# Feed-forward rows of later groups: scaling moved from VectorE to GpSimd, turning moved from TensorE to VectorE by way of DRAM

## The reference, cut to what matters

```python
x = x + xattn(layernorm(x), ctx); x = x + attn(layernorm(x))
z = layernorm(x)                       # (x - mean) / sqrt(var + 1e-5), per row of 512 channels
h = fix8(z @ w1 + b1)                  # 2048 rows, 512 -> 2048; fix8 rounds to multiples of 1/256
h = fix8(interp(h, 33 points of GELU on [-4, 4]))   # 0 below -4, h above 4
x = x + fix8(h @ w2 + b2)              # 2048 -> 512
```

## Time and profile before

| | |
|---|---|
| median of three runs | 1586.72 us |
| the profiled execution | 1586.93 us |
| its span (first to last instruction) | 1585.0 us |
| granted TensorE clock, mean | 0.999 |
| busy PE, DVE, ACT, POOL | 99%, 79%, 64%, 52% of the span |
| the feed-forward layer's rounds | from about 1216 us to the end |

### The profile page before, as it was taken

How to read it: one execution, slowest core, us unless ns; L and a number is a source line. 1 busy time by engine, 2 the same in 40 slices (tenths; PEclk the granted TensorE clock), 3 DMA queues, 4 the chain that set the end, 5 groups by cost and what they waited for, 6 DMA issues and landing times. The chain is left out here.

```text
span 1585.0 us, 30386 instructions
## 1 busy us (share of the span) xinstructions
PE 1569.8 (99%) x11114; PEld 1377.5 (87%) x11114; DVE 1245.0 (79%) x2409; ACT 1021.1 (64%) x2025; POOL 822.0 (52%) x784
## 2 busy tenths in 40 slices
PE   9999999999999999999999999999999999999998
PEld 7889899898999989999899888988988887888886
DVE  6558878887888878878788685767777889989887
ACT  3457777777777777777787442445446666666765
POOL 3318657376573856747456242333334555555554
PEclk9999999999999999999999999999999999999999
DMA  8984636456364654635433684432436601011010
GB/s 253 271 258 150 180 111 189 127 169 176 117 185 120 178 164 128 187 108 152 139 112 95 186 284 137 136 90 81 139 96 222 244 14 61 20 36 39 7 54 27
DMA packets 203412, 215.60 MB, mean 136 GB/s; under 512 B 83776, under 2 KB 149632, under 8 KB 203264
## 3 DMA queue, kind: packets, MB, share of 16 engines
q1 hardware_dynamic: 203264, 213.66, 43.8%
HBM read 154.88 MB, written 58.72 MB: 135 GB/s over the span
## 5 line engine op out<-in xcount | busy, mean ns | idle before, releaser
L79 PE MATMUL p_bank_score<-p_ctxt,p_qo 128*128 128x256 f32 x2304 | 304.6, 286 | 0.8 <-ACT p_probs L1112 0.4
L79 PEld LDWEIGHTS p_bank_score<-p_ctxt,p_qo 128*128 128x128 f32 x2304 | 288.1, 191 | 5.9 <-issue 2.2
L79 PE MATMUL p_bank_mix<-p_probt,p_ctx 128*128 128x512 f32 x1152 | 292.0, 397 | 0.5
L79 PEld LDWEIGHTS p_bank_mix<-p_probt,p_ctx 128*128 128x128 f32 x1152 | 207.4, 189 | 41.8 <-issue 3.8
L1316 DVE SCALAR_TENSOR_TENSOR p_qo<-p_bank_mix,p_odd,p_qo 128x512 fp32r<-128x512 f32 x192 | 143.8, 749 | 57.6 <-ACT p_qo L1126 50.1
L1126 ACT ACTIVATE p_qo<-p_bank_mix,p_odd 128x512 fp32r<-128x512 f32 x192 | 132.4, 690 | 68.2 <-PE p_bank_mix L79 67.6
L1112 ACT ACTIVATE p_probs<-p_bank_score,p_small 128x257 f32<-128x257 f32 x256 | 121.5, 475 | 58.6 <-DVE p_small L1297 54.1
L801 POOL TENSOR_SCALAR p_probs<-p_probs,p_small 128x256 f32<-128x256 f32 x256 | 122.2, 485 | 68.9 <-DVE p_small L1303 68.8
L795 POOL TENSOR_TENSOR p_ctx<-p_ctx_in,p_ctx 128x768 fp32r<-128x768 f32 x64 | 118.5, 1851 | 66.7 <-ACT p_ctx L1101 66.4
L790 POOL TENSOR_TENSOR p_ctx_in<-p_ctx_in,p_odd_in 128x768 f32<-128x768 f32 x64 | 118.2, 1847 | 40.2 <-DMA p_odd_in<-in_ctx_dram 40.2
L1297 DVE TENSOR_REDUCE p_small<-p_bank_score 128x1 f32<-128x257 f32 x256 | 105.4, 415 | 10.2 <-PE p_bank_score L79 7.6
(11 more groups left out here) (302 smaller groups left out, 3917.4 us busy)
## 6 DMA issues: line engine op xcount, KB each, us to landing
p_blocks_in<-in_ctx_dram SPq DMA_DIRECT2D x256, 96.0 KB, 2.4
p_ctx_in<-in_ctx_dram SPq DMA_DIRECT2D x64, 384.0 KB, 3.1
q<-p_ctx SPq DMA_DIRECT2D x64, 256.0 KB, 3.7
ffn<-p_w_raw SPq DMA_DIRECT2D x64, 256.0 KB, 2.9
p_odd_in<-in_ctx_dram SPq DMA_DIRECT2D x64, 192.0 KB, 3.6
p_x<-in_x_dram SPq DMA_DIRECT2D x32, 256.0 KB, 4.1
p_quad<-q SPq DMA_DIRECT2D x32, 256.0 KB, 3.6
p_probt<-q SPq DMA_DIRECT2D x32, 256.0 KB, 3.8
```

Of the source, the lines that this page charges most:

```text
L79: made = e.matmul(out, lhsT, rhs, start=n == 0, stop=n == last)
```

## The change

For the tiles of the later groups:

- TensorE's `turn` is gone from its list.
- GpSimd scales tile j at f = 6 + 2j (SCALED is now 6), at the head of its round, that is behind the second product of the round before. It reads the tile channel by channel of each 32-row block (every fourth element) and writes the result in order, into one of the two tiles `sums` that hold the feed-forward sums at a group's end.
- SyncE writes that tile to DRAM at f = 6 + 2j and reads it back as 4 DMAs in blocks into the place of the loaded rows.
- VectorE no longer scales; it turns the blocks with one instruction at f = 8 + 2j (TURNED is now 8), ahead of `snap`. The reading order of that instruction is contiguous (`ordered=True`); in self-attention it reads every fourth element.
- `high` and `low` follow at f = 8 + 2j.
- The statistics are finished in the same round as before (FINISHED = 5).

```diff
-    def turn_blocks(self, e, i):
+    def turn_blocks(self, e, i, ordered=False):
...
-        e.transpose(bank.rearrange("p (k a r) -> p a k r", k=C // P, r=QUAD),
-                    z.rearrange("p (a j k) -> p a k j", k=C // P, j=QUAD)).then_inc(self.turned, 1)
+        blocks = z.rearrange("p (a k j) -> p a k j" if ordered else "p (a j k) -> p a k j", k=C // P, j=QUAD)
+        e.transpose(bank.rearrange("p (k a r) -> p a k r", k=C // P, r=QUAD), blocks).then_inc(self.turned, 1)
...
-        LOADED, SCALED, TURNED = 4, 5, 7
+        LOADED, FINISHED, SCALED, TURNED = 4, 5, 6, 8
...
             def put_row(kind, i):
...
-                e.dma_start(z_dram[at, i], scaled.home(i)).then_inc(done, DMA)
+                rows = sums[i % 2][:] if kind == "n" and i >= after.early else scaled.home(i)
+                e.dma_start(z_dram[at, i], rows).then_inc(done, DMA)
...
                 if n + 7 < KF:
                     load_block(n + 7)
+                for i in tile_at(n, SCALED):
+                    put_row("n", i)
+                    load_blocks("n", i)
...
+            def scale_ordered(i):
+                x_is_in(e, "z", i)
+                if i == after.early:
+                    e.wait_ge(after.norm.steps, 14)
+                if i >= 2 * NRF:
+                    e.wait_ge(out_done, NRF * (i // NRF - 1))
+                if i >= after.early + 2:
+                    e.wait_ge(n_put, DMA * (i - 1))
+                made = x_of("z", i).rearrange("p (a j k) -> p a k j", k=KT, j=QUAD)
+                e.tensor_scalar(sums[i % 2][:].rearrange("p (a k j) -> p a k j", k=KT, j=QUAD), made,
+                                after.norm.minus[:, i:i + 1], after.norm.inv[:, i:i + 1], ALU.add,
+                                ALU.mult).then_inc(after.norm.chain, 1)
...
             for n in range(1, NF):
+                for i in tile_at(n, SCALED):
+                    scale_ordered(i)
                 rest_by_slope(n)
...
                     if k < NF - 2:
                         down(k)
-                for i in tile_at(n, TURNED):
-                    after.norm.turn(e, i)
...
-                for i in tile_at(n, SCALED):
-                    scaled_rows(i)
+                for i in tile_at(n, TURNED):
+                    e.wait_ge(n_blocks[i % 2], NB * DMA * (i // 2 + 1))
+                    after.norm.turn_blocks(e, i, ordered=True)
                 snap(n)
                 for i in tile_at(n, TURNED):
                     after.norm.low(e, i, zts_next[(g + 1) % 2], i % NRF * P)
```

More of the change, by code:

```diff
@@ L2125, in scalar @@
                 g = n // KF
-                if n == SCALED - 1:
+                if n == FINISHED - 1:
                     after.norm.root(e, 1)
@@ L2212, in low_h @@
                                            op1=ALU.subtract).then_inc(h_lo, 1)
-            def scaled_rows(i):
-                x_is_in(e, "z", i)
-                after.norm.scale(e, i, x_of("z", i))
             def down_sum(i):
@@ L2330, in vector @@
                     after.norm.guard(e, 1)
-                if n == SCALED:
+                if n == FINISHED:
                     after.norm.finish(e, 1)
```

## The result

The kernel after takes a median of 1605.51 us (1604.84 to 1605.83, 4 runs) against 1586.86 for the kernel before on the same chip: a ratio of 1.0118, 95% interval 1.0106 to 1.013. It is slower by 18.7 us. The forecast was 1596.7 and its range ended at 1604: the sign and the places of the gaps were right, the sizes not. The profiled execution took 1605.83 us, its span is 1604.0 us (1585.0 before), the granted clock 0.993 on the mean.

A forecast was written before the change was run, and what follows sets the result against it. TensorE was taken as the bound, 5.7 us to be spared; longer VectorE rounds delay the groups' first ups by 6.3, 7.6 and 10.0 us. With +10.0 us, savings included, the forecast was 1596.7 us, range 1585 to 1604.

The forecast's parts named there:

- What bounds the kernel: After 1200 us TensorE waits only 0.7 us, so sparing it the turning of 12 tiles saves at most 5.7 us.
- The turn: VectorE's added turn of 128x512 in f = 8 to 14: 0.71 us, taken as not held by GpSimd.
- GpSimd's scaling at 0.77 us: 12 scalings added on GpSimd, every fourth element read: 0.77 to 1.5 us each, taken as 0.77.
- rival C: GpSimd's strided scaling takes 1.3 to 1.5 us; a group gains 5 to 5.7 us: +16, 1603 us; chance 0.12.
- Round 6: VectorE's plain round plus a scaling on GpSimd that holds the rest and join: 6.36 us instead of 4.94.
- Even rounds: VectorE's rounds 8, 10, 12, with rest and both join instructions held by GpSimd: 7.65 us, a pair 12.26 instead of 11.46.
- rival A: Even rounds' join gets in ahead of GpSimd's first product: round 8 6.75 us, 1588.3 us in all; chance 0.21.
- The first ups: TensorE's first up of groups 1 to 3 waits for the last tile's low part: 6.3, 7.6 and 10.0 us later.
- rival D: TensorE's clock falls in each gap, first up at half rate, 2.8 us more each, 8 us: 1605 us; chance 0.08.
- The sum: Whole kernel: +10.0 us, the 5.7 us saved already taken off; median 1596.7 us.
- Hidden work: The round trip over DRAM, about 6.9 us, fits in 9.1 us between scaling and turn, with 2 us of room.
- B: GpSimd's scaling lies in a gap and holds nobody up; TensorE keeps all of 5.7 us: 1581.0 us; chance 0.14.

The follow-up runs named there:

- act_early: Kernel after, with ScalarE scaling instead of GpSimd and each group's last tile scaled at f = 11, turned at f = 13: 1586.86 us, ratio 0.9999.
- act_late_low: act_early with each tile's low part put one round later, ahead of step: 1581.27 us, ratio 0.9966.
- plain_read: Kernel after, with GpSimd scaling in order and VectorE's turn reading every fourth element: 1591.13 us, ratio 1.003.
- warm: Kernel after, with 20 matmuls whose result is thrown away ahead of each later group's first up: 1602.49 us, ratio 1.0098.
- gp_late_low: plain_read with the last tile at f = 11 and 13 and the low part one round later, ahead of step: 1581.42 us, ratio 0.9967.
- strided_late_low: Kernel after, strided scaling kept, with the last tile at f = 11 and 13 and the low part one round later: 1592.02 us, ratio 1.0032.
- act_scales: Kernel after, with the scaling given to ScalarE as two instructions (subtract in place, multiply into the ordered tile): 1586.19 us, ratio 0.9992.
- gp_scale_pe_turn: Kernel before, with only the scaling moved to GpSimd, in place and in order; TensorE still turns: 1586.46 us, ratio 0.9997.
- before_late_low: Kernel before, with the low part one round later, ahead of step; TensorE still turns: 1588.88 us, ratio 1.001.
- late_low: Kernel before, with a tile's scaling, turning and splitting one round later: 1589.6 us, ratio 1.0014.

## Why the prediction was wrong, step by step

*What bounds the kernel.* "Every microsecond that it is spared counts, as long as nothing else is late": true only by its second half. The rows had it (pairs of 11.46 against TensorE's 11.51, VectorE at its own pace), and act_early shows it. The 5.7 us are there: act_late_low takes 5.5 of them, where VectorE's group has fallen from 89.9 to 87.2, below TensorE's 88.5.

*The turn.* 0.71 us, free of GpSimd: as forecast.

*The step that failed: GpSimd's scaling at 0.77 us.* It measured 1.29. I had its bounds (0.77 and 1.5) and took the low end by the form of the instruction, though no row showed a strided read on that engine; the case was kept as rival C with 0.12. Round 6 was forecast at 6.36 and took 7.83; in plain_read, where the scaling takes 0.84, it takes 6.38, so the placing of that round was right and its input wrong. A group's gain was 5.67 us for 3.1 (C: 5 to 5.7).

*Even rounds, 7.65 forecast, 7.85 measured.* Near for a wrong reason. With a short scaling they are 7.01: the first half of `join` goes ahead of the product, which I had given to rival A. The long scaling then brought them to 7.85. So the placing was too dear by some 0.6 us a round, three times a group, and the short scaling too cheap: that the forecast came near here is luck.

*The first ups.* Round 14 was forecast at 1298.9 and started at 1301.11; tile 7's low part ended 4.2 us into it (4.3 forecast). So the step from round to `up` was right, and +6.3, +7.6, +10.0 became +8.5, +12.4, +17.2 by the rounds' length, 0.8 us of it the clock's (next paragraph).

*The clock (rival D, 0.08).* The price was right (2.4 for 2.8 us a gap), the chance far too low, and the sum had nothing for it: the forecast itself had TensorE idle for 4 to 5 us three times. But it counts once and not three times: the rows of the next group come from VectorE's rounds, which lose only 0.4 us by it. From the traces, 2.46 for the last gap (5.26 less 2.80) and what VectorE's two groups lose to the slow `up`s, 0.47 and 0.33 (95.38 and 95.24 against 94.91 in warm), give 3.3; warm gives 3.0.

*The sum.* 17.2 us for the last group's start, 2.46 for its half rate, less 0.6 by which the tail is otherwise shorter: 19.0, the growth of the span. Forecast 10.0; of the 9 us missed some 3.3 are the clock's and 5.7 are left. These 5.7 are not the price of the scaling's length, which is far higher (14.4 us from plain_read to after, 10.6 from gp_late_low to strided_late_low). With a scaling of 0.77 the forecast was 1596.7, and plain_read, with 0.84, a longer turn and two slow `up`s, takes 1591.13. So what the forecast had too dear, the placing of the even rounds above all, hid 5.6 us of the error: on the medians 14.4 less 5.6 is the miss of 8.8.

*Hidden work.* The round trip stayed hidden, no turn of the kernel after waited for a DMA. Rivals A and B fell; C and D, each priced as if alone, both came true. C's 1603 and the 2.4 that one gap's half rate costs come to 1605.4, an estimate; measured 1605.5.

## What to carry to other kernels

Before an engine is spared work, ask what the next one needs for the same stretch: where two engines both run through a stretch without waiting, moving work off one wins next to nothing until the other is shortened too. An instruction moved to GpSimd is paid in what it holds up on VectorE, so take its length for this very access pattern, bound or measure it with every stride, and look for the place where VectorE stands waiting anyway. And where a forecast lets TensorE stand for some microseconds, the half rate behind it is part of the forecast, not a rival of its own.

## What the runs showed of the hardware that was not expected

- On ScalarE, too, a read of every fourth element seems to cost: the multiplication of act_scales takes 1.22 us, the subtraction in order 0.71. The two differ in their function as well, and no run has the multiplication in order, so that the stride is the cause is likely and not shown.
- A scaling of GpSimd, one tensor input, holds VectorE's instructions with two SBUF inputs as its products do, until 0.14 us before its end (after: the scaling ends at 1255.43, the rest at 1255.98, 0.69 long by itself). The hold goes both ways: behind VectorE's `low_h` the scaling of gp_scale_pe_turn takes 1.20 us for 0.81. A turn from SBUF to PSUM is not held (after: 0.71 us from 1265.49, while GpSimd's product runs from 1265.17 to 1266.61).
- With TensorE idle for 3.7 to 4.2 us the first twelve matmuls took 5.2 to 5.5 us in every profile; behind 2.1 to 2.75 us (plain_read, before_late_low, late_low) 4.5 to 4.6, in late_low by its times in six of ten executions; behind 1.2 to 1.7 us, in three kernels, 3.0 to 3.1.
